# A decoder layer on one Trainium2 core: the first batch written out engine by engine, and a new order of the steady loop

## The reference, cut to what matters

```
x = layernorm(x + attention(x))            # 16 heads of 32, q, k, v, o each W plus a rank-16 LoRA term
x = layernorm(x + x * scan(ctx * ctx))     # r = decay * r + ctx^2 along the tokens
x = layernorm(x + ffn(x))                  # inner width 2048
ffn(x): h = gelu(silu(bitlinear(x, w1, b1)))
        h = (h - mean) / std * ln_g + ln_b
        bitlinear(h, w2, b2)
bitlinear(x, w, b): rows of x scaled by their rms and rounded to 8 bit, w rounded to -1, 0, 1 by mean|w|
```

## Time and profile before

| | us |
|---|---|
| median of three runs | 1099.99 |
| runs | 1098.48, 1099.99, 1100.02 |
| profiled execution | 1099.86 |
| its span | 1098.0 |
| PE busy | 954.8 (87%) |
| DVE busy | 896.8 (82%) |
| ACT busy | 828.9 (75%) |
| POOL busy | 591.3 (54%) |

### The profile page before, as it was taken

The page is one execution under the profiler, slowest core; times in us unless marked ns, Lnnn a source line. Parts: engine busy times, 40 slices in busy tenths (PEclk is TensorE's granted clock), DMA queues, the critical chain, the costliest instruction groups (busy, mean ns, idle before and its releaser), DMA issues.

```text
span 1098.0 us, 23490 instructions
## 1 busy us (share of the span) xinstructions
PE 954.8 (87%) x9372; PEld 656.1 (60%) x9388; DVE 896.8 (82%) x1474; ACT 828.9 (75%) x957; POOL 591.3 (54%) x767
## 2 busy tenths in 40 slices
PE   4879788998999999899989999898989899977425
PEld 2667656576766757575767657575757667554102
DVE  4476776979798989989797989889797979898676
ACT  3455677797878887787978788887878787877594
POOL 3212427556473838475564829384655748283552
PEclk9998899999999999999999999999999999998668
DMA  8504010213212231313122131323131121212204
GB/s 316 212 20 156 21 52 20 71 21 71 58 51 59 53 78 49 81 49 80 20 62 68 44 67 49 80 49 81 42 85 23 52 64 54 52 49 61 50 17 99
DMA packets 106350, 73.67 MB, mean 67 GB/s; under 512 B 91385, under 2 KB 91385, under 8 KB 104450
## 3 DMA queue, kind: packets, MB, share of 16 engines
q1 hardware_dynamic: 105522, 70.34, 23.8%
q10 hardware_dynamic: 720, 1.84, 0.5%
HBM read 41.73 MB, written 8.40 MB: 46 GB/s over the span
## 4 chain that ended last, share of the span: by engine, by line
PE 50%; DVE 31%; ACT 7%; issue 6%; DMA 4%; POOL 2%; SPq 0%; another core or an unknown queue 0%; POOLq 0%; ACTq 0%; DVEq 0%
PE bank L1255 18%; PE bank L1373 9%; PE bank L1380 8%; DVE neg_max L922 3%; PE wave L1302 3%; DVE h L1041 3%; DVE stats L971 3%; DVE fz L1046 3%; PE bank L1314 3%; PE wave L1278 2%; DMA xqT<-xq 2%; PE bank L1318 2%; DVE xq L1027 2%; PE bank L1374 2%; DVE qx L1010 2%
## 5 line engine op out<-in xcount | busy, mean ns | idle before, releaser
L922 DVE TENSOR_REDUCE neg_max<-wave 128x8 f32<-128x2048 f32 x64 | 146.2, 2284 | 61.5 <-PE wave L1278 61.5
L536 POOL TENSOR_TENSOR h<-h,g_tile 128x2048 f32<-128x2048 f32 x30 | 139.9, 4664 | 39.1 <-ACT h L726 39.1
L1373 PE MATMUL bank<-w,xqT 128*128 128x512 fp8e4 x496 | 130.4, 386 | 33.9 <-DMA xqT<-xq 25.5
L643 ACT ACTIVATE probs<-wave 128x1024 f32<-128x1024 f32 x128 | 123.9, 1020 | 31.5 <-PE wave L1302 31.4
L705 ACT ACTIVATE h<-bank,qx 128x512 f32<-128x512 f32 x124 | 84.2, 687 | 44.3 <-PE bank L1374 41.8
L432 POOL TENSOR_SCALAR attn_hi<-attn 128x256 fp32r<-128x256 f32 x64 | 26.0, 406 | 159.5 <-DVE attn L955 149.5
L1373 PEld LDWEIGHTS bank<-w,xqT 128*128 128x128 bf16 x496 | 47.0, 99 | 96.9 <-issue 25.7
L681 ACT ACTIVATE rows<-rows,rstd 128x512 f32<-128x512 f32 x96 | 74.4, 807 | 37.3 <-POOL rstd L448 15.7
L1041 DVE TENSOR_TENSOR h<-h,b_tile 128x2048 f32<-128x2048 f32 x32 | 84.0, 2624 | 18.5 <-POOL h L536 18.5
L1380 PE MATMUL bank<-w,hqT 128*128 128x512 fp8e4 x416 | 94.3, 380 | 0.0
L1255 PE MATMUL bank<-xT_hi,wq_hi 128*128 128x256 f32 x256 | 78.8, 308 | 7.8 <-DVE wk_lo L916 6.8
(11 more groups left out here) (179 smaller groups left out, 2852.0 us busy)
## 6 DMA issues: line engine op xcount, KB each, us to landing
ctx_sb<-ctxT SPq DMA_DIRECT2D x16, 512.0 KB, 3.7
rows<-x SPq DMA_DIRECT2D x16, 512.0 KB, 3.9
out<-rows SPq DMA_DIRECT2D x32, 256.0 KB, 2.1
xT_in<-xT SPq DMA_DIRECT2D x15, 512.0 KB, 4.7
h<-w1T SPq DMA_DIRECT2D x4, 1024.0 KB, 5.2
h<-w2T SPq DMA_DIRECT2D x4, 1024.0 KB, 5.6
h<-Wq SPq DMA_DIRECT2D x1, 1024.0 KB, 6.0
h<-Wk SPq DMA_DIRECT2D x1, 1024.0 KB, 9.8
```

Source lines behind the costliest of these rows:

```text
L536: po.tensor_tensor(h_of(b, q)[:, :], h_of(b, q)[:, :], g_tile[:, :], ALU.mult).then_inc(done, 1)
L643: ac.activation(probs[:, kt, :, :], wave[:, :, kt * T:(kt + 1) * T], ACT.Exp, scale=SM_SCALE).then_inc(S["probs_ready"], 1)
L922: dv.tensor_reduce(neg_max[:, :, :], wave[:, :, :].rearrange("p j (t k) -> p j t k", t=NT), axis=AX_X, op=ALU.max, negate=True).then_inc(S ...
L1373: pe.matmul(p[:, :], xqT[:, q, kc, :], w1[:, kc, n * FW:(n + 1) * FW], start=(kc == 0), stop=False)
```

## The change

1. **Loop and lead.** `body(0)` and what stood before it are replaced, on every engine, by a function `lead()` in which batch 0 and the first steps of batch 1 are written out; the loop starts at j = 1.
2. **Staging.** Wv and Wo go to `b_tile` and `g_tile` (not yet needed), so the first two chunks of the first FFN weight need not wait; the two layernorm rows are loaded once those tiles are free.
3. **Filler.** The second v product of batch 0 and the bias fold (now bank 7, in two halves) stand between other steps of batch 0; the LoRA product of o is divided 3 + 1.
4. **Second FFN weight later.** Its sums are spread over body(1); chunks 6 and 7 are rounded in body(1), 4 and 5 in body(2). The first `f` waits for the four chunks of the first weight, and `y` in body(3) for all.
5. **Steady order.** On POOL `res2` goes from behind `attn_split(j, 2)` to the next body, behind `res1`; on DVE `z_max(0)`, `z_add(1)`, `qk_lo` and `attn_norm` change places; on ACT `z_square(1)`, `ctx_square`, `normalise(3, 1)` and `v_store` move behind `probs_of(j, 3)`, and `qk_hi(j + 1, 1)` goes between the two halves of `silu`; on PE `v` is divided round `shiftT(j, 3)`, and `scores(j + 1, 0)` stands ahead of `qk(j + 1, 1)`; on SP `transpose_x` is issued ahead of `store_out(j - 3, 1)`.
6. **Banks.** `f` takes banks 6, 7 and 4 in turn, where it took 6 and 7.

The diff, cut to its core:

```diff
+        bank_no.update({("f", u): (6, 7, 4)[u % 3] for u in range(8)})
...
-        staged = {n: h[i][:, :] for i, n in enumerate("qkvo")}
+        staged = {"q": h[0][:, :], "k": h[1][:, :], "v": b_tile[:, :], "o": g_tile[:, :]}
+
+        FFW_BUFFER = (2, 3, 0, 1, 2, 3, 0, 1)
+        TERNARY_ORDER = (0, 1, 2, 3, 6, 7, 4, 5)
...
             def body(j):
                 if alive(j, 1):
                     res1(j - 1)
                 if alive(j, 2):
+                    res2(j - 2)
                     neg_mean(j - 2, 0)
...
                 if alive(j, 0):
                     attn_split(j, 2)
-                if alive(j, 1):
-                    res2(j - 1)
+                    attn_split(j, 3)
                 if alive(j, 2):
                     z_rms(j - 2, 1)
-                if alive(j, 0):
-                    attn_split(j, 3)
...
                 g_mul(PRIOR, 1)
+                res2(PRIOR)
                 res2(LAST)
...
+                if j < 3:
+                    ac.wait_ge(u_tern, (6, 8)[j - 1])
                 if alive(j, 1):
                     silu(j - 1, 0)
                 if alive(j, -1):
+                    qk_hi(j + 1, 1)
                     shiftT(j + 1, 0)
                 if alive(j, 1):
                     silu(j - 1, 1)
...
                 wait(pe, "v_stored", b, 2)
+                if c == 0 and b >= 2:
+                    wait(pe, "silu_done", b - 2, 6)
...
             def f(j, u):
 
+                if u == 2 and alive(j, 0):
+                    wait(pe, "attn_done", j, 4)
                 f_product(take(j, "f", u, "xqT_loaded", j - 1, 16), u)
...
+            def lead():
+                for m in range(3):
+                    lora_product(m)
+                lora_product(3, range(KC - 1))
+                qk(0, 0)
+                pe.wait_ge(u_merged, KC * 3)
+                scores(0, 0)
+                qk(0, 1)
...
+                v(-1, 0)
+                qk(0, 2)
+                scores(0, 1)
...
+                v(-1, 1)
+                shiftT(0, 1)
...
                 if alive(j, -1):
-                    v(j, 0)
+                    v_first_half(j, 0)
                 if alive(j, 0):
                     shiftT(j, 3)
                 if alive(j, -1):
-                    v(j, 1)
-
+                    v_second_half(j, 0)
                 if alive(j, 0):
                     shifted(j, 3)
                 if alive(j, -1):
+                    v(j, 1)
+                    scores(j + 1, 0)
+                if alive(j, 0):
+                    weighted(j, 3)
+                if alive(j, -1):
                     qk(j + 1, 1)
-                    scores(j + 1, 0)
-                if alive(j, 0):
-                    weighted(j, 3)
                 if j == 1:
-                    pe.wait_ge(u_tern, 8)
+                    pe.wait_ge(u_tern, 4)
                     pe.wait_ge(u_b1_in, 16 * NPART)
```

More of the change, by code:

```diff
@@ L193, in batches @@
         def batches(body):
-            for j in range(NB):
+            for j in range(1, NB):
                 body(j)
@@ L903, in _, with merge @@
         def _(dv):
-            def merge(m, n):
+            def merge(m, n, kcs=range(KC)):
                 dv.wait_ge(u_w[n], 16)
-                dv.wait_ge(u_merge, m + 1)
-                for kc in range(KC):
+                dv.wait_ge(u_merge, 5 if m == 3 and KC - 1 in kcs else m + 1)
+                for kc in kcs:
                     w = staged[n][:, kc * D:(kc + 1) * D]
@@ L1442, in _ @@
-            pe.wait_ge(u_lo, 2)
-            qk(0, 0)
-            lora_product(3)
-            qk(0, 1)
-            pe.wait_ge(u_merged, KC * 4)
-            scores(0, 0)
-            pe.wait_ge(u_const, 16 * 4)
-            for kc in range(KC):
-                last = pe.matmul(bank[4][:, :], bv_col[:, kc:kc + 1].to_broadcast([P, P]),
-                                 staged["o"][:, kc * D:(kc + 1) * D], start=(kc == 0), stop=(kc == KC - 1))
-            last.then_inc(u_fold, 1)
-            pe.wait_ge(u_pool, 9)
```

417 lines of the change are left out of this document (265 added, 152 removed).

## The result

The changed kernel takes **1052.93 us** (median of 4 runs, 1050.39 to 1055.55), the kernel before 1099.84 us in the same comparison: a ratio of 0.9576, with a 95% interval of 0.9551 to 0.9600, 46.9 us less. The forecast was 1051 us, 1034 to 1070. Among the runs further down, one execution of run 2 (1276.6 us) and one of run 11 (1598.1 us) had a much lower granted clock (0.73 and 0.56); they count in no ratio and shift the medians given there by less than 1 us.

A forecast was written before the change was run, and what follows sets the result against it. The steady loop was taken as bound by a ring of PE, DVE and DMA; gains of 13.1 (lead), 7.4 (body(1)), 1.9 (body(2)) and 26.6 (thirteen rings) sum to 49.0, giving 1051 us, range 1034 to 1070.

The forecast's parts named there:

- `res2` (steady order): Steady loop: moving POOL's `res2` away from quantise_x makes two small DVE instructions short again, 1.89 us less a batch.
- the lock moves with `res2`: Rival, chance 0.12: `res2` now collides with quantise_z(1) and the scan, the ring stays at 60.6, 1077 us.
- The ring of 58.6: Steady loop, one batch's PE, DVE and DMA parts in sequence: 58.6 us taken, a gain of 2.05 us a batch.
- 0.17 off: Ring's PE part: a third bank lets three `f` products go before the first `silu` is read, saving 0.17 us.
- -0.3 to +0.3: Ring's DMA part: transpose_x issued ahead of a store on SP shifts its landing by -0.3 to +0.3 us.
- The lead: Batch 0 alone at the start: reordered matmuls fill PE's waits, ending at 81 us, 13.1 less than 94.1.
- Body(1): First loop body, up to its first `f`: 48.0 us with 4.2 us of idling, gain 7.4, bounds 43.8 and 53.
- Body(2): Second loop body: two more chunks for DVE and ACT, `res2`'s 1.89 us go; 57.4 us from 59.3, gain 1.9.
- The drain: End of the run: res2(PRIOR) ahead of res2(LAST) costs 0 to 6.6 us, taken as 0.
- the slower one: Rival, chance 0.03: in-order DVE waits behind four `silu` and POOL's locks, 8.8 us later, 1111 us.
- PE as the bound: Rival, chance 0.13: nothing else waits in the steady loop, the ring is PE's own 57.45 us, 1036 us.
- the rival of the half-gained head: Rival, chance 0.13: merge, low parts and maxima keep half the head's idling, 87 lead, 53 body(1), 1064 us.

The follow-up runs named there:

- run 11: Changed kernel with the output store ahead of the transpose on SP, plus ACT's normalise(3, j-3, 1) ahead of xq_store and v_store: 1055.95 us.
- run 4: Changed kernel with the `f` products back on two accumulation banks (6, 7) and without the two waits only the third bank needs: 1066.21 us.
- run 9: Changed kernel with `res2` put back, plus 14 throw-away identity transposes on PE ahead of the first `f` in bodies 2 to 14: 1077.88 us.
- run 3: Changed kernel with SP's store of the output's second half put back ahead of the transpose of the quantised rows: 1088.16 us.
- run 12: Kernel before with `res2` moved, plus the third bank for the `f` products and its two waits: 1080.93 us.
- run 6: Changed kernel with body(1) reordered: ternary stores 2 and 3 behind the first probabilities, chunk 7's sum earlier, the second weight's total later: 1051.06 us.
- run 8: Changed kernel with both v products of batch 1 moved from batch 0's fourth-group chain to the end of the lead: 1054.06 us.
- run 5: Changed kernel with ternary(5) on DVE and its store on ACT moved to idle places in body(2): 1047.00 us.
- run 7: Changed kernel with the edits of run 5 and run 6 together: 1046.58 us.

## Why the prediction was right, and where it was not

**The parts of the ring.** Means from the traces over the rings that begin in bodies 3 to 14, in us. PE: from the first `f` to DVE's start on the second `layernorm3_sum`; DVE: from there to its last cast; DMA: from there to the next first `f`.

| | PE | DVE | DMA | sum |
|---|---|---|---|---|
| kernel before | 36.24 | 20.41 | 3.96 | 60.6 |
| the forecast's sum | 35.98 | 18.45 | 3.96 | 58.4 |
| changed kernel | 35.84 | 18.58 | 3.59 | 58.0 |
| run 1 (before, `res2` moved) | 35.87 | 18.27 | 4.60 | 58.7 |
| run 2 (after, `res2` back) | 37.34 | 20.46 | 3.60 | 61.4 |
| run 4 (after, two banks) | 36.69 | 18.61 | 3.60 | 58.9 |
| run 9 (run 2, clock held) | 35.90 | 20.42 | 3.50 | 59.8 |

**`res2` (steady order): right, shown from both sides.** Forecast 1.89 us a batch on DVE's part; it is 1.88 between run 2 and the changed kernel and 2.1 between the kernel before and run 1. The rule of the Trainium skill ("SBUF — State Buffer", section "SBUF: two separate sides"), an exclusive lock that whoever starts first keeps for its whole instruction, agrees: `ternary(5)` stood 2.9 us behind a `g_mul` begun 1.57 us earlier. It made the rival "the lock moves with `res2`" certain as a collision, and that happened, on the scan (5.59 us for 4.56). The rows had shown 4.2 us of slack for it. DVE still waits 0.83 us for the maxima behind it, so it costs nothing. One small victim is left inside the ring: the second step of `quantise_x` (L1055) takes 0.47 to 0.74 us in place of 0.16 in seven of the thirteen steady batches, with `attn_split` beside it (L1013 in the kernel before, 0.49 to 0.72 in nine).

**The ring of 58.6: 0.58 too long, and the largest share is the landing.** The sum of the parts was 58.4, from which I went up to 58.6 by the mean distance. Against 58.4 the PE part is 0.14 shorter, the DVE part 0.13 longer (the 0.2 for z_add did not show, it took 2.28 us; L1055 did) and the DMA part 0.37 shorter. In bodies 2 to 14 of the kernel before, five transposes of xq landed 4.1 to 4.6 us behind their issue and one at 3.75, the others at 3.4; in the changed kernel all landed at 3.4. The order in SP's queue is not what did it: in run 1, with the old order, and in run 3 only one of the thirteen is late. What made them late in the kernel before stays open.

**The third bank: "0.17 off" was mis-sized.** The bank is worth 0.9 us a ring in the new order (run 4) and costs 0.8 in the old one (run 12). I read its price in one batch of the kernel before (the mean there is 0.31 us), where ACT's table load came 0.4 us sooner behind the first `f`; the new order by itself makes the PE part 0.45 longer (run 4), and the bank takes back 0.85. Seen from the kernel before only 0.40 of it is left, so this large error moved the sum little.

**The transpose ahead of the store: the margin of "-0.3 to +0.3" was the wrong kind of term.** I priced the traffic. What matters is what the store waits for; behind it the old place in the new order costs 35 us (run 3), and freeing the store gives 32 back (run 11).

**The clock: missing in the forecast altogether.** The steady bodies of the changed kernel do not show it, because their gaps are 0.6 to 0.9 us. But the margin is thin: each edit that put 1.4 to 1.9 us into that gap lost another 1.6 us a batch to half-clock products (runs 2, 3), and added matmuls took it back (run 9). The Trainium skill says of it ("TensorE: Matmul & The Clock Gate", part "The HAM clock gate (the "warmup" mystery)") that activity releases the throttle; run 9 agrees, with 18 to 19 us for it.

**The lead: right** (80 against 81). PE idles 4.6 us between 18.1 and 80. **Body(1): 50.4 for 48.0**, inside its bounds. The 3.47 us for the probabilities and 3.35 us for w_sum are the idling I took at 4.2. Runs 6 and 8 show that this stretch has slack that swallows changes on either side: 5.3 us more in the lead become 1.1, and in run 6 the 6.8 us of waits turned into 4.8 us of others (2.39, 0.95 and 1.50).

**Body(2): wrong, by 6.3 us.** The step that failed: "DVE and ACT get two chunks more (about 5 and 4 us), but each is busy for only 45 of 61 us there". An engine's idle share does not say where a step may stand. Of the two chunks one stood against `g_mul` and ahead of the maxima that PE needed next; moved by a few instructions it costs little (run 5: 5.9 us back by the medians; run 7 against run 6: 4.5 us, and body(2) 58.7 us for 64.4).

**The drain: right at 0**, as the 100 us behind the last first `f` show (100 before). Rivals: the slower one needed DVE 8.8 us late; it was on time. PE as the bound came nearly true (0.8 us of idling a ring), without making 1036 us: the rings stayed 7.4 us above it and the head gained 14.8 us (208.82 - 194.01) of 22.4. That is also between the forecast and the rival of the half-gained head, but the miss lay in body(2), not in the chains that this rival named.

**The total of 1051 is right partly by luck**: body(2) and body(1) lost 8.7 us that the lead (1.1) and the rings (7.5) gave back, and of the rings' share most comes from landings that the forecast did not foresee.

The whole, from the traces: 28.3 us are `res2` (run 1). The other 18.6 are 8.9 us up to the first `f` of body(2) (202.88 in run 1, 194.01 after) and 10.1 from there to that of body(15) (764.3 against 754.2); behind it 0.4 are lost. Those 10.1 are 0.77 a ring, and without the third bank the new order's ring is 58.9 us (run 4), the old order's 58.8 (run 1): the two edits give it only together.

## What to carry to other kernels

Look for short instructions whose median is far above their minimum, and see what the other engine does at that moment: moving two GpSimd instructions was worth 28 of 47 us, and their new victim cost nothing because it had slack. Before an entry is put ahead of another on an in-order queue, ask what it waits for, not how many bytes it moves. When a reordering collects all of PE's idle time in one gap, watch the granted clock behind that gap: where it falls, a few throw-away matmuls into a bank that is overwritten anyway can be worth more than they cost.

## What was not expected of the hardware

A gap of about 2.5 us ahead of the first `f` cost more than its length: 10 us at a granted clock of 0.83 to 0.86 and about 1.6 us of time, while gaps of 0.6 to 1.2 us at this place left it at 1.00 in every run. At 1.9 to 2.1 us both were seen (1.00 in run 3 at 376.00, and in the kernel before at 452.55 and 816.99; 0.83 in run 3 at 680.90 and in run 2 at 195.51). Adding 14 transposes of 0.12 us to each of thirteen bodies made the kernel 18 to 19 us faster. In the drain 50 of them did not raise the clock for the product behind them, which still followed an idle gap of 3.95 us. Whether more of them would, was not tried.
